# Turning the attention probabilities of two early tiles by a trip over DRAM instead of on TensorE

## The reference

```python
mod = (silu(c) @ wmod).reshape(4, 6, 1, 512)
sa, ca, ga, sb, cb, gb = (mod[:, i] for i in range(6))
ga = (2 * (ga >= 0) - 1) * maximum(abs(ga), 0.25)      # gb likewise
h = layernorm(x) * (1 + ca) + sa
x = x + ga * attention(h, Wq, Wk, Wv, Wo)
h = layernorm(x) * (1 + cb) + sb
x = x + gb * (einsum('btd,rde->bte', h, factors) / sqrt(8) + bias)
```

## Time and profile before

| what | value |
|---|---|
| median of 3 runs | 464.92 us (464.91 to 466.98) |
| the profiled execution | 460.14 us |
| its span | 458.3 us |
| TensorE busy | 447.8 us, 98% |
| VectorE busy | 374.3 us, 82% |
| ScalarE busy | 336.6 us, 73% |
| GpSimd busy | 240.3 us, 52% |
| granted TensorE clock, mean | 0.993 |

### The profile page before, as it was taken

One profiled execution on the slowest core, in us unless ns is written; L12 is line 12 of the kernel. 1 busy time (PEld: TensorE's weight loads), 2 busy tenths in 40 slices (PEclk: granted clock), 3 DMA queues, 4 the chain that ended last, 5 costly groups with the idle time before them and its releaser, 6 DMA issues.

```text
span 458.3 us, 7372 instructions
## 1 busy us (share of the span) xinstructions
PE 447.8 (98%) x2116; PEld 367.0 (80%) x2116; DVE 374.3 (82%) x639; ACT 336.6 (73%) x676; POOL 240.3 (52%) x309
## 2 busy tenths in 40 slices
PE   8999999999999999999999999999999999999994
PEld 6678778888887788888888888888888887878783
DVE  5888888588877988889787987888887589998767
ACT  6799777677868697878787886878787466765570
POOL 0547446242555534555565645364654553277893
PEclk9999999999999999999999999999999999999997
DMA  8999999433587365867777366868674246568403
GB/s 301 369 302 256 200 187 177 118 102 122 171 249 231 92 199 169 247 206 237 210 201 233 93 224 197 273 192 242 196 237 118 92 149 195 177 177 268 117 23 138
DMA packets 79176, 88.07 MB, mean 192 GB/s; under 512 B 4888, under 2 KB 55832, under 8 KB 79136
## 3 DMA queue, kind: packets, MB, share of 16 engines
q1 hardware_dynamic: 75040, 79.99, 55.9%
q0 software_dynamic: 3808, 7.34, 9.2%
q10 hardware_dynamic: 288, 0.27, 0.2%
HBM read 53.49 MB, written 34.10 MB: 191 GB/s over the span
## 4 chain that ended last, share of the span: by engine, by line
PE 69%; DMA 14%; DVE 6%; ACT 4%; issue 3%; SPq 2%; POOL 1%; DVEq 0%; ACTq 0%; POOLq 0%
PE ps_o L532 8%; PE ps_o L530 8%; PE ps_o L531 8%; PE ps_v L530 5%; PE ps_v L531 5%; PE ps_v L532 5%; DMA x_blocks<-xn 5%; PE ps_y L530 4%; PE ps_y L531 4%; PE ps_y L532 4%; DMA p_blocks<-probs 3%; DMA xb<-x_blocks 3%; PE ps_s L606 2%; PE ps_qk L530 2%; PE ps_s L607 2%
## 5 line engine op out<-in xcount | busy, mean ns | idle before, releaser
L1727 POOL TENSOR_SCALAR ve<-mv 128x1 f32<-128x1 f32 x64 | 20.9, 326 | 155.0 <-DVE mv L1344 123.6
L532 PE MATMUL ps_o<-v_hi,pt_hi 128*128 128x512 f32 x192 | 74.7, 389 | 0.0
L531 PE MATMUL ps_o<-v_hi,pt_lo 128*128 128x512 f32 x192 | 74.7, 389 | 0.0
L530 PE MATMUL ps_o<-v_lo,pt_hi 128*128 128x512 f32 x192 | 74.7, 389 | 0.0
L865 ACT ACTIVATE h_f<-x1b,mod_t 128x128 f32<-128x128 f32 x120 | 53.1, 597 | 6.5 <-DVE x1b L1362 6.2
L1229 DVE TENSOR_TENSOR h_lo<-h_f,h_hi 128x512 fp32r<-128x512 f32 x57 | 41.9, 736 | 10.7 <-ACT h_hi L837 10.5
L1729 POOL TENSOR_TENSOR rstd<-ve,minus_half 128x1 f32<-128x1 f32 x64 | 44.2, 691 | 5.3
L865 ACT ACTIVATE h_f<-xb,mod_t 128x128 f32<-128x128 f32 x80 | 35.4, 594 | 12.7 <-DVE xb L1358 12.6
L530 PE MATMUL ps_v<-wvo_lo,h_hi 128*128 128x512 f32 x112 | 44.3, 396 | 0.0
L531 PE MATMUL ps_v<-wvo_hi,h_lo 128*128 128x512 f32 x112 | 43.8, 391 | 0.0
L532 PE MATMUL ps_v<-wvo_hi,h_hi 128*128 128x512 f32 x112 | 43.6, 390 | 0.0
(11 more groups left out here) (234 smaller groups left out, 1236.7 us busy)
## 6 DMA issues: line engine op xcount, KB each, us to landing
x_blocks<-xn SPq DMA_DIRECT2D x50, 256.0 KB, 2.7
p_blocks<-probs SPq DMA_DIRECT2D x24, 512.0 KB, 3.6
pb<-p_blocks SPq DMA_DIRECT2D x96, 128.0 KB, 3.2
x_ring<-in_x SPq DMA_DIRECT2D x15, 512.0 KB, 3.9
x1b<-x_blocks SPq DMA_DIRECT2D x30, 256.0 KB, 2.8
result<-x_ring SPq DMA_DIRECT2D x15, 512.0 KB, 3.0
f_sum<-in_factors POOLq DMA_DIRECT2D x14, 512.0 KB, 5.8
xb<-x_blocks SPq DMA_DIRECT2D x20, 256.0 KB, 2.9
```

The source lines that it names most:

```text
L530: nc.tensor.matmul(acc, a_hi, b_lo, start=first, stop=False)
L531: nc.tensor.matmul(acc, a_lo, b_hi, start=False, stop=False)
L532: return nc.tensor.matmul(acc, a_hi, b_hi, start=False, stop=last)
L1727: nc.gpsimd.tensor_scalar(ve[:, one], mv[:, u, 1:2], EPS, None, ALU.add).then_inc(ve_done, 1)
```

## The change

`LAST_EARLY` goes from 4 to 2. With it tiles 3 and 4 are no longer turned by TensorE but go by the trip over DRAM, every later trip uses the other half of pb or the same after two more (the trips are counted), and the scores move: tile 3's to the end of step 1 (`scored_last_in(1)` is 3), tile 4's to step 2, tile 5's to the middle of step 3. The copies of the queries of pair 2 (`queries_in`) go from the end of step 2 to the end of step 1. Since trip 0 now arrives in pb's first half while the last gate is still being made, that gate's row moves to row 2, in the second half; its making waits until the first gate, which used row 2, is stored, and tile 4's trip, into the second half, waits until it is stored itself. The store of the last gate is issued within step 2, ahead of the sending of tile 4's probabilities. ScalarE rounds h_hi of tile 11 ahead of the second pair of factor roundings.

```diff
--- before.py
+++ after.py
@@ -19,7 +19,7 @@
 BLK = P // Q
 ROW_READ = [1, 2, 3, 4, 5, 10]
 GATE_MADE = [9, 14]
-LAST_EARLY = 4
+LAST_EARLY = 2
 TILES, PER_BATCH = 32, 8
 
 
@@ -193,7 +193,7 @@
         ps_y = bank("ps_y")
         ps_qk = bank("ps_qk")
         mod_banks = [ps_s[:, 0:D], ps_s[:, D:], ps_o[:], ps_y[:], ps_o[:], ps_y[:]]
-        row_of = [0, 1, 2, 0, 1, 0]
+        row_of = [0, 1, 2, 0, 1, 2]
         low_of = [2, 3, 3, 3, 3, 3]
         sign_row = 3
         prologue_v = [ps_t[0], ps_v]
@@ -450,6 +450,8 @@
                     fetch_x(t + TB + 1, 1 - u)
                 if opening is not None:
                     send_p(opening)
+                if t == 3:
+                    sp.wait_ge(gate_stored[1], 16)
                 if t + 1 < T and not turned_by_pe(t + 1):
                     fetch_p(t + 1)
                 if 1 <= t < T - 1:
@@ -460,6 +462,8 @@
                     sp.wait_ge(w_lo_done[GB], C)
                 if 1 <= t < T - 1:
                     fetch_x1(t - 1, 1 - u)
+                if t == 2:
+                    store_gate(1, GB)
                 if scored_in(t) is not None and not turned_by_pe(scored_in(t)):
                     send_p(scored_in(t))
                 if 12 <= t + TB + 2 < T:
@@ -477,7 +481,6 @@
                 step(t)
                 if t == 2:
                     load_x(7)
-                    store_gate(1, GB)
                 if t == 3:
                     spread_gate(1, 0)
             send_p(25)
@@ -1007,6 +1010,7 @@
                 values(t + TB)
                 probs_part(t, 1)
                 if parts is not None:
+                    h_upper(q, 1 - u)
                     parts(1)
                 if t >= 2:
                     modulate_x1(t - 2, batch_of((t - 2) // 2))
@@ -1014,7 +1018,7 @@
                     normalize_x1(t - 1, 1 - u, q < T)
                 if q < T and q not in late_x_banks:
                     modulate_x_turned(q, batch_of(q // 2))
-                if q < T:
+                if q < T and parts is None:
                     h_upper(q, 1 - u)
                 if beside is not None:
                     beside()
@@ -1518,6 +1522,10 @@
                     nc.vector.tensor_scalar(mod_t[:, :, 2 * n + i, :], source, float(i), None,
                                             ALU.add).then_inc(mod_t_done, 1)
 
+            def last_row():
+                dve.wait_ge(gate_stored[0], 16)
+                row(GB)
+
             def last_vector_rests():
                 for k in range(C):
                     vector_rest(GB, k)
@@ -1615,7 +1623,7 @@
             columns(1)
             step(0, last_vector_rests, lambda: bound_gate(GA))
             dve.wait_ge(bias_loaded, 16)
-            step(1, lambda: row(GB))
+            step(1, last_row)
             step(2, lambda: bound_gate(GB))
             for t in range(3, T - TB):
                 step(t)
```

## The result

Over 20 runs of each, the changed kernel takes 468.81 us as a median (466.5 to 470.35), the kernel before 464.73 (460.87 to 469.56); the ratio is 1.0088, with a 95% interval of 1.0064 to 1.0112. It is 4.1 us slower, clear of no change. The forecast was 467.2.

A forecast was written before the change was run, and what follows sets the result against it. TensorE, busy for 98% of the span, was taken to bound the kernel. Removed −2.2, waits +4.5, then +0.3 and −0.3 gave +2.3 us: 462.4 traced, 467.2 as a median, range 463.0 to 469.0.

The forecast's parts named there:

- What is removed: TensorE in steps 3 and 4: two groups of eight transposes go, together 2.2 us.
- Waits of 0.4, 1.2 and 0.6: TensorE waits for tile 2's second pt_lo half (0.4), x tile 11's lower part (1.2), tile 3's pt_lo (0.6).
- Gate rows and SyncE: Gate instructions start at 101.0, gate store at 103.4, and x tile 12's send behind it moves from 98.92 to 104.2.
- The way back of x tile 12: Fetch to turn ahead of step 4, taken as 3.4; with 3.98 for the way out, TensorE waits 2.3.
- 0.3 in step 5: x tile 13 is late too, since each x trip waits for the one before: 0.3 more, between 0 and 0.9.
- −0.31 at 150: TensorE's wait of 0.31 at 149.99 for a lower part of x should vanish.
- the last term: The −0.3 of the sum, for the vanishing wait of 0.31 at 149.99.
- the 4.8 us carried over: Median 464.92 lies 4.8 above the traced execution's 460.14; this difference was added to the forecast 462.4.
- B: Rival: the trips are hidden and the saving stays, not slower; 462.7, or 462.4 with the 0.31; chance 0.24.
- point of decision: SyncE's send of x tile 12: if it goes out before 102.0, step 4 does not wait and B holds.
- C: Rival: the probabilities' trip is late, 10.0 instead of 8.0, moving later events by 1.6; 468.8 us; chance 0.13.
- the cover of 0.4: Tile 3's turned data arrives at 98.9, and VectorE comes to it at 99.3.

The follow-up runs named there:

- c1: The changed kernel with gate instructions between the pt_lo halves, x pair 7 loaded early, and x tile 12 sent ahead of tile 4's probabilities; 462.47 us.
- a3: The changed kernel with the last gate's store moved behind the load of x pair 7; 465.23 us.
- b1: The changed kernel with VectorE's four gate instructions of step 2 between the two halves of pt_lo; 466.66 us.
- c4: The changed kernel again, no edit, for another trace; 468.73 us.
- a4: The changed kernel with the load of x pair 7 at the head of step 2 instead of its end; 464.54 us.
- b2: The changed kernel with the edits of a4 and b1 together; 463.22 us.
- c3: The changed kernel's order of scores with tile 3 turned by TensorE, only tile 4 going by the trip; 470.75 us.
- b4: b2 with the lower part of x tile 11 made right behind the second half of pt_lo in step 2; 464.00 us.
- b3: The changed kernel with LAST_EARLY 3, so only tile 4 goes by the trip, and pair 2's queries copied at the end of step 2; 466.80 us.
- a1: The kernel before, no edit, for a second trace; its profiled execution took 467.15 us.
- c2: b4 with x tile 12 sent ahead of tile 4's probabilities in step 2; 463.26 us.

## Why the prediction was right in kind and short in size

The walk was made in the old trace's clock; the new trace runs 1.67 later from step 2 on, which is taken off in the third column.

| event | forecast | measured, less 1.67 |
|---|---|---|
| pt_hi of tile 2 | 90.6 | 90.68 |
| second half of its pt_lo | 94.75 | 94.71 |
| lower part of x tile 11 | 98.7 | 98.57 |
| turn of tile 3 | 99.3 | 99.15 |
| gate instructions | 101.0 | 100.89 |
| gate store | 103.4 | 103.20 |
| x tile 12 sent | 104.2 | 103.99 |
| pt_lo of tile 3 | 107.1 | 107.06 |
| x tile 12 fetched | 108.2 | 107.82 |
| x tile 12 turned | 111.6 | 115.06 |
| step 4's values | 115.6 | 119.03 |
| step 5 | 127.7 | 132.56 |

- **What is removed**, 2.2 us: the transposes are gone, as forecast. They are worth that only where TensorE then has work; here all of it turned into waiting. c1, with the waits of step 4 removed, gets steps 2 to 6 back to 51.8 and no lower.
- **Waits of 0.4, 1.2 and 0.6**: right. The idle times in the trace are 0.22, 0.82 and 0.52. From start to start, less the 0.23 of a matmul, they are 0.37, 0.98 and 0.68.
- **Gate rows and SyncE**: right to 0.2 us (99.3 + 1.2 + 0.6 is 101.1, not 101.0; the 103.4 goes by 101.1). That this lateness counts is seen in a3 and b1, though not by itself, since the way back got shorter in both: with the send earlier against the start of step 2 by 2.0 and by 1.4 us (15.5 and 16.1 behind it instead of 17.5) the time falls by 3.1 and by 2.0 (a3's 465.23 against 468.35, the changed kernel's median in its group; b1's 2.9 over before against 4.9). Of that, the earlier fetch is 1.45 and 0.9.
- **The way back of x tile 12** is the step that failed. I took the middle of 2.9 and 3.78, 3.4; it took 7.24 and, in c4, 6.87. The upper bound was taken from step 5 before, where probabilities and gates lie ahead too, and four fetches of probabilities directly behind the fetch at 129.98, as now:

```profile
126.48 1.01 SPq L370 DMA_DIRECT2D gates<-gate_rows  x1
...
130.41 1.80 SPq L443 DMA_DIRECT2D pb<-p_blocks  x4
```

What is not there is the load of x pair 7, 512 KB, which the change pushes from a quiet stretch into this one. I had written down that SyncE's wait holds back all behind it, and then priced the held transfers as if each still had its old surroundings. Without the load in front and with the four fetches directly behind, the way back is 3.78 here, 3.27 in a4 and 3.71 in b2; with both it is 7.24, 6.87 (c4), 6.64 (c3) and 5.31 (b1); with the load and the four fetches 4 us away, 4.50 (a3). The Trainium skill ("DMA: Bandwidth & Descriptors", issuing engines are not separate DMA queues) says that all DMAs run on the same 16 engines and interleave. The windows above agree: share 0.86 or more from 110 to 116, while the fetch was under way.
- **From step 4's values to its next product** the forecast took over the old 2.75 and put nothing down; it was 4.47, 1.7 more. 0.75 of that is ScalarE's late read of ps_y, which stands in the changed kernel as far behind step 4's first values (123.46, 2.76 behind) as in a4, where the clock was full and the product started 3.50 behind them. The other 1.0 is a lower clock (an estimate, as the difference of 4.47 and 3.50). See the last section.
- **0.3 in step 5**: no wait came there; TensorE was late enough. **−0.31 at 150**: right in direction, no wait there.
- **The sum**: steps 2 to 6 are 7.5 us longer, against the forecast's 2.6 without the last term: 3.4 more from the way back (3.8 less what earlier rows came sooner), 1.7 from ScalarE's read and the clock, −0.3. Yet the medians differ by 4.1 and 4.9, not by 7.5. In every kernel of the table that is later than before in steps 2 to 6 the medians differ by 1.4 to 3.4 us less than those steps do, and c1, equal in steps 2 to 6, is 2.3 faster. A part of that is what the kernel before loses later and the others don't: 5.6 us of waits between 150 and 400 in one of its traces, 1.0 in the other, against 2.2 and 2.3 in the changed kernel. The timed runs fit that: in the first comparison the fastest runs of the two kernels are 5.6 us apart (460.87 and 466.5), the slowest only 0.8 (469.56 and 470.35). That TensorE's lateness in step 4 is what takes those waits away is not shown: between 150 and 400 us they are 3.5 in c1, which is not late, and 0.7 to 2.8 in the kernels that are, in no order of their lateness. With two traces of the kernel before, this stays open. So two errors of mine, +4.9 in the steps and about −3 after them, partly cancelled, and the 4.8 us carried over between the profiled execution and the median hid it. That the median still came to lie below 469.0 is luck: by the steps alone it would have been 464.9 + 7.5 = 472.4.
- **The rivals**: B is refuted (the send went out 2 us behind its point of decision, and a wait of 5.5 followed). C did not occur: VectorE went from h_lo to the turn of pb at 100.82 without idle time, so the cover of 0.4 held.
- The rule that transposes of 128×128 belong on TensorE where PSUM can take them ("VectorE: DVE Perf Modes", rules for kernel authors, in the Trainium skill) agrees with the outcome for the change as written. c1 doesn't speak against it: its steps 2 to 6 are no shorter than before, and its 0.3% may come from the early load of x pair 7 or the other two edits, which the kernel before was never given.

What is shown: that the arrival of x tile 12 sets step 4 (a3, a4, b1, c1, each by another edit), and that the load of x pair 7 in front of the fetch is a large part of its lateness, 4.0 us of the way back in the changed kernel (a4) and 1.6 behind b1 (b2). Tile 4's four fetches behind it cost little where the load is away. What is only argued: what they add where it is there; a3 has 4.50 with the load still in front, but its send was earlier too.

## What to carry to other kernels

When a wait is put into a queue that issues transfers, what is behind it does not only come later: it comes together, and with what it then meets. Price each held transfer by the bytes that will be in flight beside it, not by its old duration; a transfer that nobody needs soon (here x pair 7) should be moved ahead of the wait first, and the one that the bound engine needs (here x tile 12) ahead of the bulk. Work taken off the bound engine only pays if every arrival that follows still comes in time; taking away a wait in front of a fixed arrival (b4) just moves it. And a late row delays all that stands behind it on each engine that handles it: here ScalarE's read of ps_y cost 0.75 us more, in every kernel with a wait ahead of step 4 whose clock stayed up.

## What the runs showed of the hardware that I had not expected

**TensorE's clock fell inside a kernel that is 96% busy.** Windows of the changed kernel: the wait ahead of step 4, then the matmuls behind it (granted clock is the figure behind POOL's):

```profile
114.50:120.70 6.20, 0.75 (x4) 0.28 (x2) 3.88 (x8) 3.19 (x6) 0.43 (x1) 0.73 0.57 105
120.70:122.15 1.45, 1.45 (x4) 1.16 (x4) 1.45 (x2) 1.08 (x4) 0.86 (x3) 0.50 0.46 171
```

0.50 is the lower level, 1.2 GHz, and matmuls of 512 columns start 0.43 apart instead of 0.23. In this trace the clock fell while TensorE was still waiting: it is 1.00 up to 117.00, 0.69 in the next microsecond and 0.50 in the one after. The same came with waits of 5.02 (c4), 4.74 (c3) and 2.97 us (b1) at this place, with b3's 4.38 in step 2 and with the 2.19 for pt_lo at 393.37 in a1. In b4, with 1.83, it was 1.00 to the end of the wait and fell behind it:

```profile
113.00:115.10 2.10, 0.32 (x2) 0.00 (x0) 2.02 (x6) 2.07 (x4) 0.39 (x1) 1.00 0.21 56
115.15:117.00 1.85, 1.85 (x5) 1.47 (x6) 1.85 (x3) 1.49 (x4) 0.85 (x3) 0.63 0.45 151
117.00:119.00 2.00, 2.00 (x6) 1.56 (x5) 1.81 (x5) 1.96 (x5) 0.00 (x0) 0.50 1.08 360
```

From the start of step 4's values to that of the next product it is 4.47, 5.04, 4.46, 5.29 and 4.45 us (the changed kernel, c4, c3, b1, b4), where it is 3.50 at full clock (a3, a4, b2, c2). So the lower clock cost 1.0 to 1.8 us in these five, and in b1 0.3 more in the scores.

The length of a wait doesn't decide it by itself. Behind waits of up to 1.27 us at this place (a4, a3, b2, c2), and of 1.47 and 1.51 (c3), 1.77 (b3) and 1.79 (c4) elsewhere, the clock stayed at 1.00, and it did so behind one of 2.12 us in c1, longer than b4's 1.83 (1.00 in the window from 151.94 to 156.00):

```profile
151.94 0.39 PE L534 MATMUL ps_qk<-h_lo,wqk_hi 128*128 128x256 f32 x1 [2.12 <-DVE h_lo L1234]
```

Of the waits of over 1 us between step 2 and 400 us in these thirteen traces, all of 2.19 and more are followed by the lower clock, none of 1.79 and less is, and between them both occur. The Trainium skill ("TensorE: Matmul & The Clock Gate", part 1) says that the clock is set by how busy TensorE has been recently and has two levels, which agrees with these rows.

**VectorE slowed down beside GpSimd.** The last gate instruction takes 0.68 us in the kernel before and in the changed one, and 1.67 in b1, b2, b4, c1 and c2, where GpSimd's subtractions of f_lo run at the same time; in b4 the subtraction for x tile 11's h_lo takes 1.16 in the same stretch (96.26) and in c2 1.17, where it takes 0.66 in b1 and b2, in which it starts just behind GpSimd's. All of these read two operands from SBUF; pt_lo between them, with one operand in PSUM, takes its usual 0.67. The Trainium skill ("GPSIMD Engine Reference", specifications) says that GpSimd shares its SBUF interfaces with VectorE, with contention for instructions that have two SBUF inputs, and these rows agree.
